# Storing w1's group 0 in split form within the first pair, with w2's last load and VectorE's order moved

## What is computed

```python
        w1 = W1[language_ids]
        w2 = W2[language_ids]
        h = jnp.einsum('bsh,bha->bsa', hidden_states, w1) + b1[language_ids][:, None, :]
        h = jax.nn.relu(h)
        adapted = jnp.einsum('bsa,bah->bsh', h, w2) + b2[language_ids][:, None, :]
        x = hidden_states + adapted
...
        return normed * gamma[language_ids][:, None, :] + beta[language_ids][:, None, :]
...
        h = jax.nn.gelu(jnp.einsum('bni,ih->bnh', x, W1) + b1, approximate=False)
        shared_x = jnp.einsum('bnh,ho->bno', h, W2) + b2
        expert_x = jnp.einsum('bnh,bhp->bnp', h, We_sel) + be_sel[:, None, :]
        return jnp.concatenate([shared_x, expert_x], axis=-1)
...
    x = x + _L0_cond_ref(x, itok_B_0_8, L0_cond_W1, L0_cond_b1, L0_cond_W2, L0_cond_b2, L0_cond_gamma, L0_cond_beta)
    x = x + _L1_cond_ref(x, itok_B_0_7, L1_cond_W1, L1_cond_b1, L1_cond_W2, L1_cond_b2, L1_cond_We, L1_cond_be)
```

## Time and profile before

| | |
|---|---|
| median of three runs | 1427.04 us (1427.02 to 1428.19) |
| the profiled execution | 1427.37 us, span 1425.5 us |
| PE busy | 1415.2 us (99%), 6220 products |
| DVE busy | 1011.3 us (71%) |
| POOL busy | 653.1 us (46%) |
| ACT busy | 522.9 us (37%) |
| DMA | 292.39 MB, mean 205 GB/s |

### The profile page before, as it was taken

The page is one execution under the profiler, slowest core; times in us unless marked ns, Lnnn a source line. Parts: engine busy times, 40 slices in busy tenths (PEclk is TensorE's granted clock), DMA queues, the critical chain, the costliest instruction groups (busy, mean ns, idle before and its releaser), DMA issues.

```text
span 1425.5 us, 18906 instructions
## 1 busy us (share of the span) xinstructions
PE 1415.2 (99%) x6220; PEld 1163.0 (82%) x6220; DVE 1011.3 (71%) x1645; ACT 522.9 (37%) x842; POOL 653.1 (46%) x644
## 2 busy tenths in 40 slices
PE   9999999999999999999999999999999999999999
PEld 6877878888888888888888888888888888888887
DVE  6999895776857867668677676767767687654434
ACT  4743444223442325332253323433234322432231
POOL 5987375451563514734157332564325633351101
PEclk9999999999999999999999999999999999999999
DMA  8646898457865677566774667746787457654332
GB/s 277 248 146 215 223 346 282 160 175 183 279 229 173 177 199 275 198 200 182 204 281 171 211 170 242 255 152 206 199 252 258 148 180 207 202 204 163 133 111 89
DMA packets 273957, 292.39 MB, mean 205 GB/s; under 512 B 129602, under 2 KB 230722, under 8 KB 265796
## 3 DMA queue, kind: packets, MB, share of 16 engines
q1 hardware_dynamic: 264068, 188.15, 43.9%
q10 hardware_dynamic: 9792, 103.03, 19.1%
HBM read 238.70 MB, written 52.43 MB: 204 GB/s over the span
## 4 chain that ended last, share of the span: by engine, by line
PE 89%; POOL 5%; DVE 3%; issue 2%; ACT 1%; SPq 0%; DMA 0%; DVEq 0%; ACTq 0%; POOLq 0%
PE down L275 15%; PE down L277 15%; PE down L276 15%; PE up_b L276 5%; PE up_b L275 5%; PE up_b L277 5%; PE up_c L275 4%; PE up_c L276 4%; PE up_c L277 4%; PE up_a L276 4%; PE up_a L277 4%; PE up_a L275 4%; POOL resid L1344 1%; PE aux L277 1%; PE aux L276 1%
## 5 line engine op out<-in xcount | busy, mean ns | idle before, releaser
L275 PE MATMUL down<-w,g 128*128 128x512 f32 x1024 | 399.0, 390 | 1.4 <-issue 0.6
L276 PE MATMUL down<-w,g 128*128 128x512 f32 x1024 | 398.7, 389 | 0.0
L277 PE MATMUL down<-w,g 128*128 128x512 f32 x1024 | 398.6, 389 | 0.0
L1361 POOL CAST w<-w_raw 128x256 fp32r<-128x256 f32 x125 | 70.6, 565 | 521.1 <-DMA w_raw<-m_we 521.1
L880 DVE TENSOR_TENSOR g<-g_raw,g 128x512 fp32r<-128x512 f32 x256 | 232.9, 931 | 80.0 <-ACT g L661 80.0
L275 PEld LDWEIGHTS down<-w,g 128*128 128x128 f32 x1024 | 192.3, 188 | 42.7 <-issue 1.7
L276 PEld LDWEIGHTS down<-w,g 128*128 128x128 f32 x1024 | 192.4, 188 | 39.7
L277 PEld LDWEIGHTS down<-w,g 128*128 128x128 f32 x1024 | 192.2, 188 | 39.8
L875 DVE TENSOR_TENSOR g_raw<-up_b,s 128x512 f32<-128x512 f32 x63 | 43.5, 691 | 183.0 <-PE up_b L277 170.0
L661 ACT CAST g<-g_raw 128x512 fp32r<-128x512 f32 x256 | 159.0, 622 | 8.0
L653 ACT ACTIVATE g_raw<-up_a,m_b_sb 128x512 f32<-128x512 f32 x64 | 44.1, 689 | 318.6 <-PE up_a L277 318.6
(11 more groups left out here) (225 smaller groups left out, 2506.7 us busy)
## 6 DMA issues: line engine op xcount, KB each, us to landing
w<-w_kept ACTq DMA_DIRECT2D x55, 1792.0 KB, 7.5
w<-w_kept SPq DMA_DIRECT2D x56, 768.0 KB, 5.0
w_raw<-m_we SPq DMA_DIRECT2D x128, 128.0 KB, 4.6
out<-resid SPq DMA_DIRECT2D x64, 256.0 KB, 4.4
xTs_raw<-xT SPq DMA_DIRECT2D x56, 256.0 KB, 3.0
xs<-x SPq DMA_DIRECT2D x56, 256.0 KB, 7.0
w_kept<-w SPq DMA_DIRECT2D x8, 1792.0 KB, 8.0
x_turned<-turned SPq DMA_DIRECT2D x112, 128.0 KB, 3.3
```

The lines of the kernel that those rows point to most:

```text
L275: eng.matmul(bank, a_hi, b_hi, start=opens, stop=False, skip_group_check=True)
L276: eng.matmul(bank, a_hi, b_lo, start=False, stop=False, skip_group_check=True)
L277: return eng.matmul(bank, a_lo, b_hi, start=False, stop=closes, skip_group_check=True)
L1361: eng.tensor_copy(hi, values).then_inc(pool_eh[b], 1)
```

## The change

**Group 0 of w1.** The quarters A11, A12 and A22, split at the start of pair 0 for step 0, are stored at once to w1_kept (`keep_first_w1`), ahead of the next raw load into that buffer, which now waits for these stores. In step 4 SyncE loads all four quarters of group 0 once more, into `parts`, a tile that lies over t1; GpSimd makes S1 to S4 in step 5 (`pool_first_sums`) into `sums`, which lies over b12; ScalarE rounds them in step 6 into `sums_hi` (over t1) and GpSimd makes `sums_lo` (over b12). SyncE stores them in step 6 with four issues (`keep_sums`). t1 and b12 are otherwise first written with the T1 and the B12 of pair 1, and B12's load waits for the stores. In step 7 the raw load of group 0, its sums, its rounding, VectorE's `dve_rest_w1_lo` (L1035), GpSimd's share (L1326) and the store at the end of the pair are gone. ScalarE's queue loads group 0 from w1_kept instead, in step 7 ahead of B11's rounding.

**SyncE in step 7.** w2's raw load and the experts' loads of group 7 now stand behind B12 and ahead of B22 and B21.

**VectorE in pair 0.** Step 3: the low half of C12's g of group 2 stands behind w1's low half, no longer ahead of u2; w2's low half stands ahead of c22. Step 4: the low half of C22's g of group 3 stands behind the adapter sums. Step 6: the second turns stand ahead of w1's low half. Step 7: B11's low halves stand behind c12 and c22, ahead of them before.

```diff
+    sums_hi = sb("sums_hi", [P, 4, 2 * P], f32r, "t1")
+    sums_lo = sb("sums_lo", [P, 4, 2 * P], f32r, "b12")
+    parts = sb("parts", [P, 4, 2 * P], f32, "t1")
+    sums = sb("sums", [P, 4, 2 * P], f32, "b12")
...
     def pe_p1(eng, i, m, k):
-        if i is pairs[1] and k == 0:
-
-            eng.wait_ge(pool_w1, 3)
-        elif i is not first:
-            eng.wait_ge(in_w1[k % 2], i.count(8 * GROUPS, 16 * (k // 2 + k % 2) - 8 * GROUPS))
+        if i is not first:
+            eng.wait_ge(in_w1[k % 2], i.count(8 * GROUPS, 16 * (k // 2 + 1) - 8 * GROUPS))
...
+    def act_sums_hi(eng):
+        eng.wait_ge(pool_w1, 6)
+        eng.copy(sums_hi[:, :, :], sums[:, :, :]).then_inc(act_first_w, 1)
...
+            if k == GROUPS - 1 and i is first:
+                load_w1(eng, m, 0)
             if k == GROUPS - 1:
                 for c in range(2):
                     act_block_hi(eng, m, B11, c)
...
-        if i is first:
+        if i is first and k < GROUPS - 1:
             act_w1_hi(eng, k + 1)
...
+    def pool_first_sums(eng):
+
+        p11, p12, p21, p22 = (parts[:, n, :] for n in range(4))
+        s4, s1_, s2_, s3_ = (sums[:, n, :] for n in range(4))
+        eng.wait_ge(in_first_w, 48)
+        eng.tensor_tensor(s1_, p21, p22, ALU.add).then_inc(pool_w1, 1)
+        eng.tensor_tensor(s3_, p11, p21, ALU.subtract).then_inc(pool_w1, 1)
+        eng.wait_ge(pool_w1, 3)
+        eng.tensor_tensor(s2_, s1_, p11, ALU.subtract).then_inc(pool_w1, 1)
+        eng.wait_ge(pool_w1, 5)
+        eng.tensor_tensor(s4, p12, s2_, ALU.subtract).then_inc(pool_w1, 1)
+
+    def pool_sums_low(eng):
+        eng.wait_ge(act_first_w, 3)
+        eng.tensor_tensor(sums_lo[:, :, :], sums[:, :, :], raw(sums_hi[:, :, :]), ALU.subtract).then_inc(pool_w1, 1)
...
         if k == 2:
             eng.wait_ge(pe_first, 4)
+            eng.wait_ge(kept_first, 32)
...
+    def keep_first_w1(eng):
+
+        eng.wait_ge(pool_w1, 2)
+        for of in (slice(A11, A12 + 1), slice(A22, A22 + 1)):
+            eng.dma_start(raw(w1_kept[0, :, :, of, :]), raw(w1[:, 0, :, of, :])).then_inc(kept_first, 16)
...
+    def keep_sums(eng):
+
+        eng.wait_ge(pool_w1, 7)
+        for part, source in ((HI, sums_hi), (LO, sums_lo)):
+            eng.dma_start(raw(w1_kept[0, :, part, S4, :]), raw(source[:, 0, :])).then_inc(kept_first, 16)
+            eng.dma_start(raw(w1_kept[0, :, part, S1:S3 + 1, :]), raw(source[:, 1:4, :])).then_inc(kept_first, 16)
 
     def load_w1(eng, i, k):
-        eng.wait_ge(kept_w1[k % 2], 8 * GROUPS)
+        if k == 0:
+            eng.wait_ge(kept_first, 96)
+        eng.wait_ge(kept_w1[k % 2], 16 * (GROUPS // 2 - 1 + k % 2))
```

More of the change, by code:

```diff
@@ L799, in act_step @@
         act_first_sum(eng, i, k)
+        if i is first and k == 6:
+            act_sums_hi(eng)
         if i is first and k % 2 == 1:
@@ L1135, in dve_first_step @@
                 dve_t1(eng, m, c)
+        if k > 2:
+            dve_sum_c12(eng, i, k)
+        if k == 3:
+            dve_w2_lo(eng, k - 1)
+        dve_sum_c22(eng, i, k)
+        if k == GROUPS - 1:
             for c in range(2):
                 dve_b_lo(eng, m, B11, c)
[L1138 to L1144, removed]
         dve_g_lo(eng, i, k, C11)
@@ L1155, in dve_first_step @@
             dve_g_lo(eng, i, k - 1, C22)
+        if k == 4:
+            dve_g_lo(eng, i, k - 1, C22)
+        if k == 6:
+            dve_turns(eng, m, 1, 2)
         if k < GROUPS - 1:
             dve_w1_lo(eng, k + 1)
-            if k == 6:
-                dve_turns(eng, m, 1, 2)
+            if k == 3:
+                dve_g_lo(eng, i, k - 1, C12)
             if k == 5:
@@ L1318, in pool_first_w1_lo @@
     def pool_first_w1_lo(eng, n):
[L1320 to L1325, removed]
+        s = slice(n * A22, n * A22 + 2)
+        eng.wait_ge(act_first_w, n + 1)
         eng.tensor_tensor(w1[:, 0, LO, s, :], w1_raw[:, 0, LO, s, :], raw(w1[:, 0, HI, s, :]),
@@ L1420, in pool_first_step @@
             return
+        if k == 6:
+            pool_sums_low(eng)
         pool_roots(eng, m, k)
@@ L1519, in load_first_aw @@
         halves = slice(0, D // 2), slice(D // 2, D)
-        for s, landed in zip(halves, (in_aw[0][0], in_first_aw)):
+        for s, landed in zip(halves, (in_aw[0][0], in_first_w)):
             eng.dma_start(aw_tile(first, 0, 0)[1][:, LO, s], a_w1[language, :, s]).then_inc(landed, 16)
@@ L1588, in keep_w1, with load_parts @@
         eng.wait_ge(dve_w1, k)
-        if k == GROUPS:
-            eng.wait_ge(pool_w1, 3)
-        eng.dma_start(raw(w1_kept[k % GROUPS, :, :, :, :]), raw(w1[:, k % 2, :, :, :])).then_inc(kept_w1[k % 2], 16)
+        eng.dma_start(raw(w1_kept[k, :, :, :, :]), raw(w1[:, k % 2, :, :, :])).then_inc(kept_w1[k % 2], 16)
+    def keep_first_w1(eng):
+        eng.wait_ge(pool_w1, 2)
+        for of in (slice(A11, A12 + 1), slice(A22, A22 + 1)):
+            eng.dma_start(raw(w1_kept[0, :, :, of, :]), raw(w1[:, 0, :, of, :])).then_inc(kept_first, 16)
+    def load_parts(eng):
+        eng.wait_ge(dve_t, T_ORDER.index((T3, 1)) + 1)
+        eng.wait_ge(pool_tlo, T_ORDER.index((T1, 1)) + 1)
+        for n, of in enumerate((0, GROUPS)):
+            eng.dma_start(parts[:, 2 * n:2 * n + 2, :], m_w1[of, :, :].rearrange("p (a n) -> p a n", a=2)).then_inc(in_first_w, 16)
+    def keep_sums(eng):
[3 more added lines that the diff above has]
+            eng.dma_start(raw(w1_kept[0, :, part, S1:S3 + 1, :]), raw(source[:, 1:4, :])).then_inc(kept_first, 16)
     def load_w1(eng, i, k):
-        eng.wait_ge(kept_w1[k % 2], 8 * GROUPS)
+        if k == 0:
+            eng.wait_ge(kept_first, 96)
+        eng.wait_ge(kept_w1[k % 2], 16 * (GROUPS // 2 - 1 + k % 2))
         eng.wait_ge(pe_p[4], seven(i, k - 1))
@@ L1639, in load_blocks @@
             eng.wait_ge(dve_t, m.count(8, 0))
+            if m is pairs[1]:
+                eng.wait_ge(kept_first, 96)
         elif of == B11:
@@ L1740, in sp_pair @@
                 load_blocks(eng, m, B12 if i is first else B11)
+                if i is first:
+                    load_w2_raw(eng, k)
+                    load_experts(eng, k, experts)
                 load_blocks(eng, m, B22)
```

32 lines of the change are left out of this document (17 added, 15 removed).

## The result

The changed kernel takes **1433.14 us** (median of 6 runs, 1432.29 to 1433.72) against 1427.60 (6 runs, 1427.02 to 1428.19) for the kernel before: ratio 1.0039, 95% interval 1.0026 to 1.0052. It is 5.5 us slower where +1.0 was forecast, and above the stated range (1423.8 to 1430.9). The profiled run took 1433.1 around a span of 1431.3.

A forecast was written before the change was run, and what follows sets the result against it. The prediction took TensorE's work plus a few microseconds of waiting in pair 0 as the bound. VectorE's q +2.0 and T3's pair -1.0 gave +1.0 on 1427.04: 1428.0 us, range 1423.8 to 1430.9.

The forecast's parts named there:

- VectorE's shorter row: End of pair 0: without group 0's low half (2.46 us) VectorE would be 2.4 us sooner, if nothing else bound it.
- the sum for the landing of group 7's store: Pair 0 to 1: 196.5 + 3.2 + 1.5 - 1.2 = 200.0 us, bounds 197.1 to 203.9; VectorE's q follows, +2.0 us.
- The lead, -1.2: Steps 3 and 4 of pair 0: u2 comes sooner, taking 1.2 us off the store's landing; bounds 0 and 4.1.
- The sums' stores, +1.5: Step 6: four stores, 1.05 MB, ahead of the turned stores, 2.6 to 3.3 us with 1.1 free; taken as +1.5.
- Group 0's load, +3.2 net: Step 7: 1.84 MB loaded in place of 0.52 MB of raw parts; net 1.31 MB, 3.2 us at 407 GB/s.
- Rival B: Step 7: group 0's load goes ahead of B12, landing at 189.6 instead of 185.1; slower, 1430.4 us; chance 0.18.
- T3's pair, -1.0: Step 0 of pair 1: T3's two subtractions, 2.38 us beside GpSimd's T2 pair, run alone in 1.28: -1.0 us.
- The order in this row, not its length: VectorE, step 7: moving B11's low halves behind c12 and c22 changes the row's order but not its length.
- Rival A: Pair 0 to 1: the store lands no later than 196.5, VectorE's row binds q, gain 3.3 us, 1423.7; chance 0.14.

The follow-up runs named there:

- e1: Changed kernel with ScalarE's load of w1's group 1 issued behind B22's two roundings in step 0 of pair 1: 1428.72 us.
- e5: Changed kernel with VectorE's order of the kernel before in steps 3, 4, 6 and 7 of pair 0: 1433.38 us.
- e4: Kernel before with only VectorE's new order in steps 3, 4, 6 and 7 of pair 0: 1426.60 us, ratio 0.9994.
- e6: Changed kernel with the four stores of the sums made twice, 1.05 MB more ahead of the turned stores: 1436.05 us.
- e12: Changed kernel with the load of w1's group 0 for pair 1 cut to one of fourteen slices (0.13 MB): 1428.92 us.
- e9: Changed kernel, ScalarE's group 1 load behind B22's roundings, SyncE's order B12, w2's raw load, group 0, B22, B21: 1425.87 us.
- e11: Changed kernel with the load of w1's group 0 for pair 1 bringing only the high halves (0.92 MB): 1431.81 us.
- e7: Changed kernel with w2's raw load of group 7 back behind B22, B21 and the store of w2's group 6: 1433.02 us.
- e10: As e9, but with the load of w1's group 0 last, behind B22 and B21: 1430.24 us.
- e2: Changed kernel with the load of w1's group 0 on SyncE's queue behind B12, instead of ScalarE's: 1434.21 us.
- e3: Changed kernel with the edits of e1 and e2 together: 1427.90 us, ratio 1.0003.

## Why the prediction was wrong

Right was the mechanism: a lead in steps 3 and 4 that TensorE keeps in part, no gain from VectorE's shorter row, and the end set by ScalarE's load of group 1, queued behind group 7's store, with s, q and T2 behind it. e1 takes the wait away and 4.2 to 4.4 of 5.5 us go. The sign of the forecast and the place stand; what failed is the sum for the landing of group 7's store: **200.0 forecast, 204.4 measured** (bound: 203.9). Counted from 81 us the landing is 8.25 us later than before, where the sum had 3.5, so 4.75 were missed. By its terms:

- **The lead, -1.2: wrong for the transfers.** Product for product TensorE is 0.4 us ahead at 81 us, which is the shift, 1.9 at 98 us, 0.1 behind at 115.5 (the 1.5 us wait on g, as argued) and 1.2 ahead after step 4. Less the shift the lead there is 0.8 us, just what I had worked out for the second adapter product; the other 0.4 of my 1.2 had no row. But the store of step 5 is issued at 152.74, before 152.63. Counted from 81 us it is 0.5 us later in the changed kernel, 0.4 in e5 and 0.1 in e4, and earlier in none. SyncE waits there for VectorE's turns (6.2 us, before 5.7), not for TensorE. I subtracted a TensorE lead from a SyncE time without asking whom that queue waits for: -1.2 forecast, +0.5 measured, 1.7 us.
- **The sums' stores, +1.5: mis-sized.** I counted room in 170 to 173 us as available. In the changed kernel it is not there, and the stretch behind is less full than before instead (share 0.78 against 0.96). Its stretches (length, clock, DMA share, GB/s):

```profile
170.00:173.00 3.00, 1.00 1.01 260
173.00:176.00 3.00, 1.00 0.78 111
```

  Measured: 2.1 us at w2's raw load, counted from 81 us and less the 0.5 above, and 1.9 to 2.9 by e6. The price without the room, 2.6 to 3.3, was nearer: 0.4 to 1.4 us.
- **Group 0's load, +3.2 net: the saving that I took off did not come.** The load is a block, a stretch in which little else moves, worth 4.3 us of the landing by e12 (204.4 against 200.65, and e12's run was 0.6 us late at 81 us), of which half the bytes give back 1.5. While it ran, the turned stores' 128-byte packets got about a turn for a turn at best; SyncE's next issues stood for 3.7 and 3.4 us, and B11 and B12 came behind. At 407 GB/s the whole 1.84 MB would be 4.5 us, so the load itself was rightly sized. The 0.52 MB of raw parts seem to have saved nothing: B12's chain of store, landing and load leaves the engines room there. The same stretch in the kernel before, and then in e12, which has no raw parts and one slice of the load:

```profile
180.00:185.00 5.00, 1.00 1.09 302
```

```profile
180.00:185.00 5.00, 1.00 0.91 200
```

  This second point is argued from the rows, no run tried it. Together 1.1 us more than taken. Lead, sums and load make 3.2 to 4.2 of the 4.75 us, and 0.6 to 1.5 stay unassigned.
- **Rival B: its place and its rule were right**, B12 at 191.3 even past its 189.6. One mistake was to make it and the forecast exclusive. Both waits occurred, one behind the other, and the block went into the store's landing too. Its price was wrong as well: with B12 as late and the store's wait gone (e1), q starts at 200.86 and not past 203, since VectorE's row from T1's start to q is 9.9 us, where before it was 14.7 and I took off only 2.4.
- **T3's pair, -1.0: right.** 1.28 us as forecast. It is 1.28 in e1 too, where nothing is held up, so the hold-up that I gave as the reason is not needed for it. Half a microsecond of it goes again behind u2, in the T4 pair.
- **"The order in this row, not its length": wrong, without effect here.** In e4, which has the new order and every operation of before, T1's start to q is 13.6 us against 14.7; the low half of L1035 takes 1.23 us there and not 2.46.
- **No gain without the wait:** with it gone (e1) the kernel is still 1.4 us over its before; Rival A's 1423.7 was not reached even in e9, where VectorE's row, 3.3 us earlier at u2, gives TensorE only 1.7.

The Trainium skill (DMA: Bandwidth & Descriptors, on queues, rings and completion order) says that a DMA engine takes turns between its queues packet by packet. From 181 to 184 us the trace agrees, 78 turns against 76, if a packet is one row of the pattern. In other runs SyncE's queue got fewer turns with stores issued and not yet moved: 76 against 15 in e5 over the same stretch, 78 against 8 in e11 over 181 to 183; why is open. I had worked out from the rule that B12 "would share", which would need packets of equal size. By the rows above a row of 14,336 bytes holds one engine for 0.6 us and one of 128 for 0.013, so even a turn for a turn gives Rival B's result. So the rule did not speak against Rival B; my use of it did.

The Trainium skill has on the same page, under its rules for kernel authors, that a second issuing engine adds no bandwidth. The trace agrees: 293 GB/s over 177 to 197 us, 321 before.

## What to carry to other kernels

A transfer put on a second queue does not fill the holes of the first: in these traces the queues took about a turn for a turn at best, so a load of 14 KB rows held up stores of 128-byte pieces that had already been issued, for as long as it ran. Put behind the transfers that were wanted next and close to its own deadline (e9), it cost 0.9 us of waiting, and the whole kernel lost nothing. Where an engine issues a transfer that must wait for another transfer, move it behind the work that others want (e1: 4.2 to 4.4 us for three lines). And a time won on one engine is carried over to a queue only after finding whom that queue waits for.

## What had not been expected of the hardware

TensorE's clock. After the pause of 3.3 us the granted clock fell to the 1.2 GHz level: products start 0.43 us apart from 207.15 to 214, where 0.23 is usual.

```profile
204.00:207.00 3.00, 0.00 (x0) 1.00 1.06 319
207.00:214.00 7.00, 6.04 (x14) 0.52 1.00 380
214.00:217.00 3.00, 2.67 (x12) 0.98 0.55 212
```

It was seen again after pauses of 3.4 (e11), 3.5 (e5), 3.7 (e7) and 4.1 us (e10), and in e2 (5.1 us, clock 0.80 over 200 to 225); the kernel before, e1, e3 and e9, whose longest wait here is 1.5 us, kept 1.00 in their profiled runs (other runs of the kernel before have a mean of 0.998 over the whole span, the same as the changed kernel). But the length of one pause does not sort the runs: in e6 the clock was at the lower level over 212 to 218 us after a pause of 2.1, and in e12 over 208 to 210 after waits of 0.3, 0.3 and 1.2 close together (in e5 a second time, over 212 to 214, after 0.2, 0.3 and 1.2), while a pause of 1.2 in the kernel before left it full. It cost nothing in the changed kernel: VectorE's four low halves ran for 6.8 us at the same time, and against e1, with full clock, u2 is 4.65 us later and the span 4.7 us longer.
